# Turning the order of the groups in a routed MLP with LayerNorm: a long group last of the whole ones, and VectorE seeding the last banks

## The reference

```python
out_nr  = gelu(x @ w1_nr + b1_nr) @ w2_nr + b2_nr            # condition 0: 256 -> 256 -> 256
out_tsr = gelu(x @ w1_tsr + b1_tsr) @ w2_tsr + b2_tsr        # condition 1: the same sizes
h = gelu(x @ w1_sr + b1_sr)                                  # condition 2: 256 -> 512
h = gelu(h @ w2_sr + b2_sr)                                  #              512 -> 256
out_sr = h @ w3_sr + b3_sr                                   #              256 -> 256
y = x + where(c == 0, out_nr, where(c == 1, out_tsr, out_sr))
mu, var = mean(y), mean((y - mu) ** 2)                       # over the 256 features
result = (y - mu) * rsqrt(var + 1e-5) * gamma + beta
```

## Time and profile before

| | us |
|---|---|
| median of 3 runs | 102.68 |
| lowest and highest run | 101.89, 102.86 |
| the profiled execution | 102.77 |
| its span | 101.1 |
| TensorE busy | 83.8 (83%) |
| VectorE busy | 76.8 (76%) |
| ScalarE busy | 66.6 (66%) |
| GpSimd busy | 64.0 (63%) |
| granted clock of TensorE, mean | 0.969 |

### The profile page before, as it was taken

One profiled execution on the slowest core, in us unless ns is written; L12 is line 12 of the kernel. 1 busy time (PEld: TensorE's weight loads), 2 busy tenths in 40 slices (PEclk: granted clock), 3 DMA queues, 4 the chain that ended last, 5 costly groups with the idle time before them and its releaser, 6 DMA issues.

```text
span 101.1 us, 1747 instructions
## 1 busy us (share of the span) xinstructions
PE 83.8 (83%) x502; PEld 73.1 (72%) x502; DVE 76.8 (76%) x209; ACT 66.6 (66%) x108; POOL 64.0 (63%) x81
## 2 busy tenths in 40 slices
PE   0239999999999999999999999999999999960000
PEld 0137588887886988879989899898988999950000
DVE  5578966849775504985799999899999999899900
ACT  0667046999599503599999899998998990800000
POOL 7918605005977760040567898998889989899900
PEclk9999999999999999999999999999999999999755
DMA  0892899810028999300000220402205005051570
GB/s 0 261 358 47 284 336 321 207 17 0 0 47 311 281 366 409 152 0 6 0 0 6 89 122 6 183 5 96 118 0 208 6 0 214 0 182 39 208 242 20
DMA packets 5782, 13.01 MB, mean 129 GB/s; under 512 B 656, under 2 KB 3104, under 8 KB 5760
## 3 DMA queue, kind: packets, MB, share of 16 engines
q0 software_dynamic: 2672, 9.57, 25.8%
q1 hardware_dynamic: 3068, 3.15, 10.3%
q10 hardware_dynamic: 20, 0.01, 0.0%
HBM read 8.53 MB, written 4.46 MB: 129 GB/s over the span
## 4 chain that ended last, share of the span: by engine, by line
PE 57%; DVE 15%; POOL 10%; ACT 5%; DMA 4%; issue 4%; DVEq 0%; POOLq 0%; ACTq 0%
PE ps_f L1045 14%; PE ps_x L962 7%; PE ps_a L985 7%; PE ps_a L990 6%; PE ps_a L986 6%; DMA xs<-x_dram,load_idx 4%; POOL rstd L456 2%; PE ps_b L1130 2%; PE ps_a L1130 2%; PE ps_b L1127 2%; PE ps_b L1126 2%; PE ps_a L1127 2%; PE ps_a L1126 2%; POOL xs L467 2%; POOL xs L472 2%
## 5 line engine op out<-in xcount | busy, mean ns | idle before, releaser
L985 PE MATMUL ps_a<-x_hi,w_lo 128*128 128x512 f32 (+1 forms) x40 | 16.3, 409 | 0.0
L467 POOL TENSOR_TENSOR xs<-xs,gamma_b 128x768 f32<-128x768 f32 (+1 forms) x7 | 12.4, 1778 | 5.3 <-ACT xs L567 5.1
L986 PE MATMUL ps_a<-x_hi,w_hi 128*128 128x512 f32 (+1 forms) x40 | 15.1, 381 | 0.0
L1045 PE MATMUL ps_f<-wf_lo,f_hi 128*128 x60 | 15.1, 283 | 0.0
L1045 PE MATMUL ps_f<-wf_hi,f_hi 128*128 x60 | 15.0, 283 | 0.0
L564 ACT ACTIVATE ps_a<-ps_a,bias_cols 128x512 f32<-128x512 f32 (+1 forms) x22 | 14.3, 648 | 0.0
L563 ACT ACTIVATE f_hi<-ps_a,bias_cols 128x512 fp32r<-128x512 f32 (+1 forms) x16 | 10.6, 665 | 4.8 <-PE ps_a L1130 4.8
L421 POOL DMA_INDIRECT xs<-x_dram,load_idx x10 | 10.4, 1040 | 5.0 <-issue 2.6
L456 POOL TENSOR_TENSOR rstd<-var_eps,half 128x4 f32<-128x4 f32 (+1 forms) x9 | 9.1, 1007 | 6.9 <-DVE var_eps L787 6.7
L472 POOL TENSOR_TENSOR xs<-xs,beta_b 128x768 f32<-128x768 f32 (+1 forms) x7 | 12.4, 1769 | 0.1
L990 PE MATMUL ps_a<-x_lo,w_hi 128*128 128x512 f32 (+1 forms) x40 | 12.1, 384 | 0.0
(11 more groups left out here) (168 smaller groups left out, 200.6 us busy)
## 6 DMA issues: line engine op xcount, KB each, us to landing
w_raw<-L_cond_w_sr_dram SPq DMA_DIRECT2D x2, 512.0 KB, 4.4
wf_raw<-L_cond_w_sr_dram SPq DMA_DIRECT2D x1, 256.0 KB, 5.1
w_raw<-L_cond_w_tsr_dram SPq DMA_DIRECT2D x1, 256.0 KB, 5.8
w_raw<-L_cond_w_nr_dram SPq DMA_DIRECT2D x1, 256.0 KB, 6.1
...
xs<-x_dram,load_idx POOLq DMA_INDIRECT x10, 7.3
...
```

The costliest lines, as they stand in the source:

```text
L467: nc.gpsimd.tensor_tensor(tiles, tiles, spread(gamma_b, n), ALU.mult).then_inc(gam_pool, 1)
L985: nc.tensor.matmul(dst, w1_lo[:, kt, cols], xh[:, kt, :], start=(kt == 0), stop=False)
L986: nc.tensor.matmul(dst, w1_hi[:, kt, cols], xh[:, kt, :], start=False, stop=False)
L1045: return nc.tensor.matmul(ps[:, b, t * H:(t + 1) * H], stationary[:, kt, (2 * b + t) * P:(2 * b + t + 1) * P], weights[:, bass.ds(f_at + k ...
```

## The change

- **Order.** Slot s holds group s+1 for s = 0 to 6, and slot 7 holds group 0. With these inputs: long, six short, long, half. Slots 0 to 6 (`SURE`) can be filled without knowing the number of groups; the slots behind them (`late_rows`) have a small product and two index ops of their own, and their gathers wait for them. Four gathers instead of three come ahead of `wf_lo`.
- **Last layer inside layer 1.** In a long step TensorE now does layer-1 blocks 0 and 1 (`long_first`), the last layer of the slot before, and then blocks 2 and 3 (`long_rest`) and the second layer.
- **VectorE and ScalarE** do a long group's second-layer ops at the start of the next step (`low_second`, `gelu_second`), and `middle`/`normed` behind block 1 of a long group instead of behind block 3.
- **The end.** x + bias of slot 7 goes into `ps_f`, and that of the half group into `ps_a[1]`, by a VectorE op each (`with_x`), and the last layer is added to them; `bias_and_x` is gone there. The half group's second layer-1 block uses `ps_z`, and waits for `gamma_beta_one(6)`. Of slot 7's tiles, 0 and 1 are normalized by ScalarE and GpSimd, 2 and 3 by VectorE. The moments of slot 7 are taken bank by bank.

```diff
+            for s in range(EARLY, SURE):
+                gather(s)
+            pool.wait_ge(late_idx_done, 2)
+            for s in range(SURE, SLOTS):
...
             def pool_half(g):
-
-                times_gamma(g - 2, 2, TT)
-                plus_beta(g - 2, 2)
-                root(g - 1)
+                times_gamma(g - 2, POOL_TT, TT)
+                plus_beta(g - 2, POOL_TT)
                 scatter(g - 2, False)
-                root(g, HTT)
-                scatter(g - 1, True)
+
+                root(g - 1, g, slice(0, 2))
+                shifted(g - 1, slice(0, 2))
+                root(g - 1, g + 1, slice(2, TT))
+                times_gamma(g - 1, 2, 2)
+                root(g, g + 2, slice(0, HTT))
+                plus_beta(g - 1, 2)
+
+                scatter(g - 1, False, 2 * (g + 1))
...
             def act_half(g):
                 f = f_hi[g % 2]
+                normed(g - 2)
+                gelu_second(g - 1)
                 bias_at = act.snap((cls[g].with_bounds(min_val=HALF_TSR, max_val=HALF_NR) - 2) * 4)
-                for m in range(2):
-                    gelu(ps_a[m][:, 0, 0:HTT * P], f[:, m, 0:HTT * P], bias_cols[:, bass.ds(bias_at + m, 1)],
+                for m, bank in ((0, ps_a[0]), (1, ps_z)):
+                    gelu(bank[:, 0, 0:HTT * P], f[:, m, 0:HTT * P], bias_cols[:, bass.ds(bias_at + m, 1)],
                          HID * g + SHORT[m], SHORT_STEP[m])
-                normed_shared(g - 2)
+
+                act.wait_ge(rstd_done, g)
+                for t in (0, 1):
+                    z(g - 1, t, xs[g - 1][:, t, :], ps_f[:, 0, t * H:(t + 1) * H])
                 store_half_part(act, seq_regs, taken_regs, g, HPER // 2)
...
+            nc.vector.tensor_reduce(groups[:, :], kinds[:, 0:ROUTES], AX.X, ALU.add).then_inc(dve_step, 1)
+            step[0] += 2
+            dve.wait_ge(consts, CONSTS)
             dve.wait_ge(dve_step, step[0])
+            chain(nc.vector.scalar_tensor_tensor(out=next_group[:, :], in0=slot_id[:, :], scalar=groups[:, 0:1],
+                                                 in1=slot_id[:, :], op0=ALU.is_lt, op1=ALU.add))
+            chain(nc.vector.scalar_tensor_tensor(out=group_id[:, :], in0=slot_next[:, :], scalar=groups[:, 0:1],
+                                                 in1=next_group[:, :], op0=ALU.not_equal, op1=ALU.mult))
+            chain(nc.vector.tensor_tensor(
+                ended[:, :, :],
+                group_id[0:1, :].rearrange("b (s r) -> b s r", r=1).broadcast_to([1, GROUPS, ROUTES + 2]),
+                ends[:, :].rearrange("b (s r) -> b s r", s=1).broadcast_to([1, GROUPS, ROUTES + 2]), ALU.is_ge))
...
+                def with_x(ps, x_tiles, route, n):
+
+                    b_at = dve.snap(route * H)
+                    nc.vector.tensor_tensor(
+                        ps, x_tiles,
+                        bias_b[:, bass.ds(b_at, H)].rearrange("p (a h) -> p a h", a=1).broadcast_to([P, n, H]),
+                        ALU.add).then_inc(x_seeded, 1)
+
+                def half_with_x():
+                    dve.wait_ge(low_done, HID * (g - 1) + HID - 1)
+                    with_x(ps_a[1][:, 0, :].rearrange("p (t h) -> p t h", t=HTT), xs_half[:, :, :],
+                           cls[g].with_bounds(min_val=HALF_TSR, max_val=HALF_NR) - 2, HTT)
 
                 def next_stats(b):
-
                     dve.wait_ge(f_ready, 2 * (g - 1) + b + 1)
                     for t in (2 * b, 2 * b + 1):
                         nc.vector.bn_stats(stats[:, t, :], next_tile(t)).then_inc(bn_done, 1)
 
+                with_x(ps_f[:, :, :].rearrange("p b (t h) -> p (b t) h", t=2), xs[g - 1][:, :, :],
+                       cls[g - 1].with_bounds(max_val=NR), TT)
+
+                with dve.If(cls[g - 1] < TSR):
+                    low_second(g - 1, 0)
+                    gamma_beta_one(g - 2)
+                    half_with_x()
+                    low_second(g - 1, 1)
+                with dve.Else():
+                    gamma_beta_one(g - 2)
+                    half_with_x()
+
+                for m, bank in ((0, ps_a[0]), (1, ps_z)):
+                    low(bank[:, 0, 0:HTT * P], f[:, m, 0:HTT * P], f_l[:, m, 0:HTT * P],
+                        HID * g + SHORT[m], SHORT_STEP[m])
+
+
                 next_stats(0)
-                for m in range(2):
-                    low(ps_a[m][:, 0, 0:HTT * P], f[:, m, 0:HTT * P], f_l[:, m, 0:HTT * P],
-                        HID * g + SHORT[m], SHORT_STEP[m])
-                gamma_beta_shared(g - 2)
+                bank_moments(g - 1, ps_b, 0)
                 next_stats(1)
-                moments(g - 1, ps_b)
-                dve.wait_ge(mv_done, g)
-                times_gamma_first(g - 1, next_tile, TT, u_next)
+                bank_moments(g - 1, ps_b, 1)
                 dve.wait_ge(f_ready, 2 * g + 1)
                 for t in range(HTT):
                     nc.vector.bn_stats(stats[:, t, :], half_tile(t)).then_inc(bn_done, 1)
-                moments(g, ps_b, HTT)
-                root_and_beta(g - 1, next_tile, xs[g - 1], TT, u_next)
+                moments(g, ps_x, HTT)
                 dve.wait_ge(mv_done, g + 1)
-                times_gamma_first(g, half_tile, HTT, u_last)
-                root_and_beta(g, half_tile, xs_half, HTT, u_last)
+                times_gamma_first(g - 1, next_tile, (2, 3), u_next)
+                dve.wait_ge(mv_done, g + 2)
+                times_gamma_first(g, half_tile, range(HTT), u_last)
+                root_and_beta(g, half_tile, xs_half, range(HTT), u_last, g + 2)
+                root_and_beta(g - 1, next_tile, xs[g - 1], (2, 3), u_next, g + 1)
...
+            def norm_first(s):
                 if s == 1:
                     dve.wait_ge(places_ps, 1)
                     nc.vector.tensor_copy(place_tab[:, :, :], places_pt).then_inc(place_tab_done, 1)
                 if s >= 1:
                     middle(s - 1)
+
+            def norm_second(s):
+                if s == 0:
+                    bias_parts()
...
             def half_first(route, g):
                 pe.wait_ge(w_lo_done, L1_WAIT[route])
-                for m in range(2):
-                    pe.wait_ge(low_done, HID * (g - 1) + SHORT[m])
-                    layer1(l1_cols(route, m), g, ps_a[m], SHORT_STEP[m], HTT * P)
+                pe.wait_ge(low_done, HID * (g - 1) + SHORT[0])
+                layer1(l1_cols(route, 0), g, ps_a[0], SHORT_STEP[0], HTT * P)
+
+                pe.wait_ge(o_dve, 2 * (g - 1))
+                layer1(l1_cols(route, 1), g, ps_z, SHORT_STEP[1], HTT * P)
 
             def half_group(g):
-                route = cls[g].with_bounds(min_val=HALF_TSR, max_val=HALF_NR) - 2
+                route = cls[g - 1].with_bounds(max_val=NR)
+                half_route = cls[g].with_bounds(min_val=HALF_TSR, max_val=HALF_NR) - 2
                 pe.wait_ge(x_lo_done, upto_x(g))
                 with pe.If(cls[g] < HALF_NR):
                     half_first(TSR, g)
                 with pe.Else():
                     half_first(NR, g)
-                next_to_last(g - 1)
-
-                pe.wait_ge(y_done, g - 1)
-                last_layer_and_x(g, ps_f, route, 1)
+
+
+                f_at = pe.snap(route * (KT * H))
+                pe.wait_ge(gelu_done, HID * (g - 1) + HID)
+                pe.wait_ge(x_seeded, 1)
+                for b in range(2):
+                    last_products(g - 1, ps_f, f_at, b, True)
+                f_at = pe.snap(half_route * (KT * H))
+                pe.wait_ge(gelu_done, HID * g + HID)
+                pe.wait_ge(x_seeded, 2)
+                last_products(g, ps_a[1], f_at, 0, True)
...
                     last_layer(s - 1)
                 with pe.If(cls[s] < TSR):
+                    long_rest(s)
                     long_second(s)
```

185 lines of the change are left out of this document (112 added, 73 removed).

## The result

| | before | changed |
|---|---|---|
| median, us (22 runs each) | 102.58 | 101.97 |
| lowest and highest | 101.83, 103.61 | 100.86, 102.82 |
| profiled execution | 102.77 | 102.46 |
| its span | 101.1 | 100.4 |
| time around the span | 1.67 | 2.06 |

The ratio is 0.9937, with a 95% interval of 0.991 to 0.9963. The change gives 0.6 us where 2.9 were forecast, and 101.97 lies in what the prediction itself calls "same" (101.7 to 103.7), to which it gave 0.11. A second series of the changed kernel gave 101.42 (10 runs) beside 102.48 for the kernel before, ratio 0.99 (0.9859 to 0.9942), and its profile is of an execution of 101.01. The first profile, at 102.46, is among the slower executions of the kernel, so both are read: what differs between them is not the change.

A forecast was written before the change was run, and what follows sets the result against it. TensorE was taken as full to 90 us, VectorE as the limit of the last 15. Last scatter at 92.5 plus 5.7 gave span 98.2; with 1.67 around it 99.9, by the median 99.8; range 98.6 to 102.0.

The forecast's parts named there:

- The chain through the step and the half group: End: the half group's second layer-1 block waits for `gamma_beta_one(6)` to free `ps_z`, a TensorE stall of 1.2 us.
- The steps and the two gaps: TensorE: short steps at 6.55 us each, then waits of 0.2 in the last long step and 1.2 at the half group.
- Step 1: First of the six short steps: began at 26.51 before, forecast to start at 26.8.
- step 7: The long group's step after six short ones: VectorE's low part fits by 0.2; if 0.4 late, TensorE stands 0.2.
- Scatter of group 7 at 92.5: End: the last scatter starts 0.2 us behind VectorE's last tiles, which end at 92.3.
- I take 5.7: End: time from the last scatter's start to the span's end, 5.7 us, bounds 5.4 and 6.0; 6.0 before.
- +1.67 around the span: Outside the span: the 1.67 us of the profiled execution before, added to the forecast span of 98.2.
- The front: Before the short steps: the additional small product for the late slots on TensorE's way, +0.3 us, bounds 0 and 0.6.
- The contention: End: VectorE's two SBUF-input additions contend with GpSimd, taking up to 1.7 times as long; 0.3 us would reach the end.
- A part of it is given back: Rival, short steps: VectorE needs 0.2 to 0.4 us more per step, TensorE waits; 101.0 to 102.2; chance 0.17.
- It does nothing: Rival, order: reordering only shifts the queue, VectorE's work after TensorE's last product stays 11 us; 101.1; chance 0.03.
- Slower: Rival, step branches: each jump makes VectorE stand 0.81 us, six steps cost 4.9, net +4.3, 104.2; chance 0.08.

The follow-up runs named there:

- second profile: The kernel before with four more semaphores that nothing uses, profiled again: 102.68 us, span 101.0.

## Why the prediction was wrong, step by step

It was within its range, at the edge of it, and wrong in size: a gain of 0.6 us (1.1 in the second series) where 2.9 was forecast. The medians are 102.0 and 101.4 where 99.8 was. The chain through the step and the half group was right; what failed are the terms behind VectorE's last operation, the start of the last scatter first of all.

- **The steps and the two gaps** were right, and so was TensorE's last product (87.79 in the quiet execution; 87.7 to 88). Step 1 starts at 26.69 in the quiet execution (forecast 26.8), a short step takes 6.5, the gap in step 7 is 0.34 (0.2), that at the half group 1.19 (1.2), VectorE's last operation ends at 92.27 (92.3). The chain through `gamma_beta_one(6)`, `ps_z` and the half group was the real one.
- **"Scatter of group 7 at 92.5 (it began 0.2 behind what released it)"** is the step that failed. The 0.2 was read where GpSimd's own root came last, and the root hid the DMA's preparation. In the changed kernel VectorE comes last, and 0.80 pass: +0.6, in both profiles and in the four relatives that keep this hand-over. Letting GpSimd come last again gave 1.1 us back.
- **"I take 5.7"**, with bounds 5.4 and 6.0, from there to the end of the span: 5.8 in the quiet execution, 6.8 in the other, and 5.9, 6.3, 6.3, 6.4 and 6.7 in the five relatives without the stall in which the scatter waits for VectorE too. The middle one is 6.3: +0.6. One scatter does not land faster than two (4.4 and 5.4 to landing, 4.4 before); the gain of 0.3 from its being alone was not there, and the 6.0 of before was one draw as well (6.4 in its second profile).
- **"+1.67 around the span"** is 2.06: +0.4. I had carried it over as a constant, and nothing in the profile speaks of it.
- **The front**, +0.3 with bounds 0 and 0.6: 0.18 and 0.75 in the two profiles against the one of before, whose first transposes took 1.35. Like against like it is 0.4, so the term was nearly right. But the transposes take 1.06 to 1.71 from one execution to the next, and step 1 starts at 26.6 to 27.3 with them.
- For the quiet execution the terms sum to 0.6 + 0.1 + 0.4 = 1.1, and 99.9 + 1.1 = 101.0 (101.01 measured). With the middle value behind the scatter it is 0.6 + 0.6 + 0.4 = 1.6, and 99.8 + 1.6 = 101.4, the median of the second series. The last 0.6 up to 102.0 in the first series is about what slow first transposes cost. This part is an estimate: only one execution of each series has a profile.
- **The contention** was costed at up to 0.3 to the end, and costs nothing there in the changed kernel: no wait of TensorE ends with it. Its mechanism was mis-stated as a factor.
- **The rivals.** "A part of it is given back" gave the right time (101.0 to 102.2) for a wrong reason: the period of the short steps is no longer than before. "It does nothing" has 101.1 and is as near; the old order at 109.46 refutes it. "Slower" by a stall at a branch does not describe the changed kernel in these runs, but the time of five of its relatives, 104.7 to 107; 0.08 was not too much. Its evidence was misread, though. The 0.81 at 34.65, with "issue" to blame, begins 0.03 behind the end of ScalarE's GELU (33.97 + 0.65 = 34.62), and in the second profile of before the same wait, 0.82, is put down to that GELU. The unexplained wait in that trace was the one of 3.8 us at L766, which the prediction passes over.
